# A four-layer graph network on one core: attention columns loaded ahead of the first basis group, and their semaphore awaited behind both zeroing products

## The reference, cut to what matters

```
edge_index = jnp.stack([src, dst])
h = relu(layernorm(x)); x = x + L0(h, edge_weight, ...)     # two GCN layers: A_norm @ h @ W_gcn @ W_mlp
h = relu(layernorm(x)); x = x + L1(h, edge_index, ...)      # four conditioned attention blocks
h = relu(layernorm(x)); x = x + L2(h, edge_index, ...)      # diffusion over the adjacency, three steps
h = relu(layernorm(x)); x = x + L3(h, src, dst, type, ...)  # two relational layers
# L3, for each of its two layers: the weights of both relations are mixtures of 30 bases
w = jnp.einsum('rb,bio->rio', att, basis)                   # att (2, 30), basis (30, 512, 512)
```

## Time and profile before

| | |
|---|---|
| Runs (median, and all three) | 902.92 us (902.92, 903.7, 899.2) |
| Profiled execution, span | 898.7 us |
| PE busy | 842.5 us, 94% of the span |
| DVE busy | 560.8 us, 62% |
| ACT busy | 398.6 us, 44% |
| POOL busy | 230.9 us, 26% |
| DMA | 113.39 MB, mean 126 GB/s |

### The profile page before, as it was taken

How to read it: one execution, slowest core, us unless ns; L and a number is a source line. 1 busy time by engine, 2 the same in 40 slices (tenths; PEclk the granted TensorE clock), 3 DMA queues, 4 the chain that set the end, 5 groups by cost and what they waited for, 6 DMA issues and landing times. The chain is left out here.

```text
span 898.7 us, 13977 instructions
## 1 busy us (share of the span) xinstructions
PE 842.5 (94%) x4222; PEld 637.2 (71%) x4223; DVE 560.8 (62%) x1221; ACT 398.6 (44%) x646; POOL 230.9 (26%) x253
## 2 busy tenths in 40 slices
PE   4999789999789999999997999999999979799998
PEld 2666556767567778777694777877777857488786
DVE  6999987658956666477655575674766636620110
ACT  3999893234435612356223365134561325431210
POOL 4000022208512123401254022343212404413200
PEclk9999999999899999999998999999999989899999
DMA  7999924524245643537533346535366386130100
GB/s 169 201 215 238 271 49 128 155 76 128 94 117 119 181 107 115 138 99 193 133 114 90 97 98 189 132 118 135 86 183 156 106 225 173 31 94 0 47 12 35
DMA packets 37846, 113.39 MB, mean 126 GB/s; under 512 B 5908, under 2 KB 6472, under 8 KB 30108
## 3 DMA queue, kind: packets, MB, share of 16 engines
q1 hardware_dynamic: 20604, 79.00, 36.7%
q10 hardware_dynamic: 17184, 33.69, 10.9%
HBM read 105.33 MB, written 7.34 MB: 125 GB/s over the span
## 5 line engine op out<-in xcount | busy, mean ns | idle before, releaser
L690 POOL TENSOR_TENSOR wl<-wraw,wh 128x512 fp32r<-128x512 f32 x140 | 179.7, 1318 | 412.7 <-ACT wh L768 379.3
L1806 PE MATMUL ring<-ohs,ohd 128*128 128x512 f32 x312 | 79.7, 408 | 6.4 <-DVE ohs L1317 6.4
L1806 PEld LDWEIGHTS ring<-ohs,ohd 128*128 128x128 f32 x312 | 59.1, 194 | 31.3 <-issue 18.6
L1295 DVE SCALAR_TENSOR_TENSOR ohd<-iota,dstT,vals 128x256 fp32r x156 | 69.8, 481 | 7.9 <-PE ring L1806 4.5
L768 ACT ACTIVATE wh<-wraw 128x2048 fp32r<-128x2048 f32 x35 | 66.9, 1910 | 8.4 <-PE ring L1704 5.0
L793 ACT ACTIVATE yT_h<-ring 128x512 fp32r<-128x512 f32 x32 | 19.1, 597 | 99.6 <-PE ring L1722 99.6
L817 ACT ACTIVATE ohs<-iota,minus_srcT 128x512 fp32r<-128x512 f32 x78 | 52.4, 713 | 16.1 <-PE ring L1806 9.6
L1733 PE MATMUL mix_ps<-quad,att_shift 120*32 120x512 f32 x384 | 52.5, 623 | 7.4 <-DMA quad<-in_L_gnn_basis 7.4
L695 POOL TENSOR_TENSOR rstd<-ve,half 128x1 f32<-128x1 f32 x44 | 24.1, 551 | 105.3 <-DVE ve L1146 105.0
L1704 PE MATMUL ring<-yT_h,wh 128*128 128x512 f32 x128 | 49.8, 389 | 0.0
L1704 PE MATMUL ring<-yT_l,wh 128*128 128x512 f32 x128 | 49.8, 389 | 0.0
(11 more groups left out here) (382 smaller groups left out, 2159.8 us busy)
## 6 DMA issues: line engine op xcount, KB each, us to landing
quad<-in_L_gnn_basis SPq DMA_DIRECT2D x60, 960.0 KB, 8.0
wraw<-in_L_gnn_m_w ACTq DMA_DIRECT2D x8, 1024.0 KB, 6.0
mix_scratch<-mixed SPq DMA_DIRECT2D x128, 32.0 KB, 4.0
wraw<-in_L_gnn_wv ACTq DMA_DIRECT2D x4, 1024.0 KB, 5.3
wraw<-in_L_gnn_wq ACTq DMA_DIRECT2D x4, 1024.0 KB, 5.2
wraw<-in_L_gnn_wk ACTq DMA_DIRECT2D x4, 1024.0 KB, 5.4
wraw<-in_L_gnn_wo ACTq DMA_DIRECT2D x4, 1024.0 KB, 5.3
wraw<-mix_scratch ACTq DMA_DIRECT2D x4, 1024.0 KB, 5.7
```

Of the source, the lines that this page charges most:

```text
L690: last = g.tensor_tensor(wl[s][:, k, :], wraw[s][:, k, :], wh[s][:, k, :].bitcast(F32), ALU.subtract)
L1295: return v.scalar_tensor_tensor(out, at.unsqueeze(1).broadcast_to([P, 4, HALF]), dstT[:, e], vals[:, e, :].rearrange("p a b -> p (a b)").u ...
L1806: last = te.matmul(ring[:, banks[b], :], ohd[:, s, b, :], ohs[:, s, :], start=False, stop=False)
```

## The change

The four `att` loads move ahead of group 0 on SP, and the first group is issued in the loop with the other three. On TensorE the second `zero` moves ahead of the waits for `flags_ready` and `att_step` 3. No instruction is added or removed.

```
             sp.dma_start(eint[:, 0, :], src_d.rearrange("(t p) -> t p", p=P)).then_inc(edges_loaded, 16)
-            load_pass_group(0, 0)
             for l in range(2):
                 for r in range(2):
                     sp.dma_start(att[0:QUADS * BASES, l, r:r + 1], ...).then_inc(att_loaded, 16)
-            for k in range(1, GROUPS):
+            for k in range(GROUPS):
                 load_pass_group(0, k)
             sp.wait_ge(const_ready, 2)
...
             zero(0, True)
+            zero(1, True)
             pe.wait_ge(flags_ready, 1)
             pe.wait_ge(att_step, 3)
-            zero(1, True)
             with pe.Fori(0, NT) as m:
```

## The result

The changed kernel takes 902.83 us (median of 20 runs, 901.67 to 904.99). The kernel before, on the same chips, takes 901.24 us (20 runs, 898.56 to 903.70). The ratio of the two is 1.0023, with a 95% interval of 1.0013 to 1.0033. That is 1.2 to 3.0 us, well under 0.5%, but more runs than before tell it from nothing. The forecast of 902.8 us was met and what it stood for, an exchange without loss, was not.

The account below looks back on a forecast made before the run. TensorE, busy 94% of 898.7 us, was taken as the bound, its late start pacing the edge stage. -2.3 at the start and +2.3 at group 4 gave 0.0; with 4.2 from span to median, 902.9, rounded to 902.8; range 898.9 to 904.9.

Parts of the forecast that it names:

- an exchange without loss: At group 4's start: 2.3 us gained at the first group, given back waiting for group 4, net 0.0 us; chance 45%.
- When the columns land: On SP's queue: four `att` loads at 1.6 us each end at 9.3, the last landing at about 9.8 instead of 12.6.
- The first group: TensorE's first mixing group starts at about 14.7 instead of 17.03, waiting for group 0's transfer, 2.3 us gained.
- Everything behind is 2.0 us later.: On the DMA queue: group 1 lands at 19.4 instead of 17.4, and group 4 at 38.5 instead of 36.5.
- the 21.57 us from there: TensorE's time from first group to group 4, 38.60 - 17.03 in the kernel before, so it would want group 4 at 36.3.
- From there the distance from group to group is TensorE's own work, 4.85 a group, and nothing later is changed.: On TensorE from group 4's start at 38.6: groups follow at 4.85 us as before, with no further gain or loss.
- the rival on the clock: A 2.3 us TensorE wait at group 4 lowers its clock behind it: slower by up to 1.7 us, 904.6; chance 15%.
- Quick columns: Column loads take 1 us each or less, group 4 lands before 36: faster by 2 to 3.5 us; chance 25%.
- the figure of the Trainium skill: Fixed cost of about 2 us per transfer: the last column, issued at 4.36, would land near 6.4.
- The late stream: Columns end later than 9.3, so TensorE waits longer at group 4: slower by up to 1.7 us, 904.6; chance 15%.
- The sign set for this: In the changed trace, a fifth group starting after 39 would show the columns slower than 1.6 us a load.

Follow-up runs that it names:

- the doubled run: The changed kernel with the four column loads issued twice, the second time into unused memory, all eight ahead of group 0: 907.27 us, 1.0067 to the kernel before.
- the moved loads alone: The kernel before with only the four column loads moved ahead of group 0, the second zeroing product staying behind the waits: 902.67 us, ratio 1.0025.
- the filled wait: The changed kernel with ten zeroing products on TensorE right before its wait for group 4: 901.26 us, ratio 1.0007 to the kernel before.
- spread in both kernels: 31 small loads moved back, 12 behind group 6 and 19 behind group 10: on the changed kernel 897.42 us, 0.9966; on the kernel before 902.36 us, 1.0011.
- the split columns: The changed kernel with only layer 0's two columns ahead of group 0, layer 1's behind group 3: 901.01 us, ratio 0.9999 to the kernel before.

## Why the prediction was wrong

**The number.** That 902.8 was met is luck. The forecast stood on the median of three runs, 902.92, and twenty runs put it at 901.24; this error of 1.7 us covered the loss of 1.6. The predicted change was nothing, and the measured one is 1.2 to 3.0 us.

**When the columns land.** Forecast 9.8, measured 9.3. The landings are at 4.9, 6.0, 7.1 and 9.3: 1.1 us a load, and 2.2 for the last. The group behind the last seems to lengthen it: in the doubled run, where more columns follow, the fourth lands 1.25 us behind the third. The single packets of the idle stretch show the pace, here from 5 to 6 us:

```profile
DMA packets 120, 0.00 MB, mean 0 GB/s; under 512 B 120, under 2 KB 120, under 8 KB 120
```

At 120 a us and some 138 packets a load that is 1.15 us, against the 1.6 that I took from the earlier trace rows; the doubled columns say 1.2. That the 74 packets in 1.6 us in the earlier trace rows were the end of one load and not the pace of the next is my reading, and no run shows it. But the trace of before had a better row than packets: its four columns landed at 9.48, 9.99, 11.28 and 12.61, 1.3 us apart for the last two. The price was too high by a third, and the step came out nearly right only because the end of the last is longer: luck again.

**The first group.** Forecast 14.7 behind group 0's transfer, measured 14.31 behind it. The mechanism was right and its size nearly so. POOL ended at 11.3 and not at 12.9, since its four pieces took 1.75 us and not the 3.04 of the earlier trace rows, but nothing waited for it.

**"Everything behind is 2.0 us later."** This is the first step that failed. I measured the delay at one place, group 1, and carried it through. It was 1.6 us there (19.0 against 17.4), less than forecast. But it grew: group 3 is issued at 8.10 in both kernels and lands 19.6 us later before and 22.4 after, the rows here.

```profile
mask<-in_L_gnn_basis SPq DMA_DIRECT2D x1, 960.0 KB, 19.6
```

```profile
mask<-in_L_gnn_basis SPq DMA_DIRECT2D x1, 960.0 KB, 22.4
```

Group 4 is 2.8 us late as well. TensorE reached its wait at 36.5, 0.2 us later than forecast: it started 0.4 us earlier, but the 21.57 us from there, taken over from the kernel before, were 22.2, because full pace came later behind the start. The wait was 2.8 us and not 2.3, and the start at 39.34 is 0.74 late instead of 0.0.

**"From there the distance from group to group is TensorE's own work, 4.85 a group, and nothing later is changed."** This is the second step that failed, and the larger one. The distance was 6.45 once. I had the mechanism, with its place and a price of up to 1.7 us (measured 1.6), as the rival on the clock, and gave it 15%, since one case is no rule. The fault was in how the cases were set up: the likeliest one itself contained a new wait of 2.3 us, longer than the 1.88 us that had cost the clock once. So the rival was not an alternative to the exchange but its consequence. Added to it, the forecast would have been +0.0 + 1.7, close to the 2.3 us of the trace and the 1.6 between the medians.

The sum of the two, 0.74 + 1.60 = 2.34 us at the sixth group, is what the trace shows (45.79 against 43.45), and on the chip the moved loads alone show the two together, and the filled wait takes the second away and leaves the first.

**The other rivals.** Quick columns did not happen, though 1.1 us a load is close to the 1 us that this rival asked for: the first group still waited for group 0, since a queue that is quick per load still carries four of them. By the figure of the Trainium skill that the prediction held against its row ("DMA: Bandwidth & Descriptors", Latency and other measured facts: a fixed cost of about 2 us) the last column, by an estimate, would have landed some 2 us after its issue; it took 4.7, and the measurement decides. The late stream happened, by 0.74 us, but not by its own condition: the last column landed at 9.3, before the forecast 9.8. The sign set for this, a fifth group after 39, thus pointed at slow columns where the delay had grown further down the stream.

**What stays open.** Why group 3 was delayed by 2.8 us where group 1 was by 1.6. The small loads are not the reason, though group 3 lands 0.8 to 1.2 us earlier without them in either order: with them spread in both kernels, group 3 lands at 26.5 with the columns behind group 0 and at 29.7 with them ahead, 3.3 us apart, and group 1 at 17.5 and 19.0, 1.5 apart. While group 4 was under way, from 32 to 36 us, the transfers moved 260 GB/s before and 198 after; why is open. Why TensorE came to full pace later in the changed kernel is open too. Also that the clock stood at half for 6.8 us in the split columns and for 3.4 in the changed kernel, after waits of 2.68 and 2.81 us.

## What to carry to other kernels

When an edit brings an early start and delays a stream, follow the stream to the first transfer that has little slack; the gain is given back there, and it is better to take other work off the queue ahead of that transfer together with the edit. A forecast that ends in "it only waits elsewhere" must price what that wait does to TensorE's clock, in the same case and not in another; here that was 1.6 us once and 2.8 another time, for waits of nearly the same length. A tiny load of single elements is a large one for the queue: it is to be counted in packets and not in bytes.

## What the runs showed of the hardware that was not expected

- A load of 0.5 KB in 120 single elements takes 1.1 to 1.2 us of an otherwise idle queue, a quarter of what a group of 960 KB takes (4.7 us), and what stands behind it is later by that much, or more further down the stream.
- The same loads on a second queue, beside the groups, took 16.0 us (median) from issue to landing, against 3.1 to 4.7 alone.
- POOL's four `att_shift` pieces took 1.74 to 1.75 us in all runs where they began at 8.6 to 10.1 or at 25.7, and 3.04 to 3.60 where they began at 12.8 to 13.3, when VectorE was making one-hots. With half the columns the two pieces of layer 1 took 11.35 us from 27.53 on, when VectorE made one-hots without a pause until 38.1, and the two of layer 0 took 1.03 us at 8.5. That VectorE slows them is likely, and was not tried by itself.
- A wait of 2.8 us of TensorE was followed by half the clock for 3.4 us; 2.4 us of useless products in the same wait kept the full clock. A wait of 2.7 us was followed by 6.8 us of half the clock.
- At the start of the stage eight mixing products took 1.94 us, as they do where the granted clock reads 0.50 (the fifth group with half the columns), while it read 1.00. A granted clock of 1.00 in the first 20 us is to be checked against the duration of the products.
